# Moving a mixture's shared expert from the attention loop into the loop over the experts

## The reference

```python
x = hidden_states.reshape(T, H)
topk_idx, topk_w = _route(x, gate_weight, e_bias)
...
out = jax.ops.segment_sum(vals * flat_w[:, None], flat_t, num_segments=T)
shared = jax.nn.silu(x @ shared_gate.T) * (x @ shared_up.T) @ shared_down.T
return (out + shared).reshape(B, S, H)
```

## Time and profile before

| what | value |
|---|---|
| median of 3 runs | 1954.37 us (1952.79 to 1955.15) |
| the profiled execution | 1958.1 us, span 1956.3 us |
| PE busy | 1732.0 us, 89% of the span |
| PE weight loads | 1372.8 us, 70% |
| DVE busy | 1408.1 us, 72% |
| ACT busy | 1149.3 us, 59% |
| POOL busy | 568.1 us, 29% |

### The profile page before, as it was taken

One profiled execution on the slowest core, in us unless ns is written; L12 is line 12 of the kernel. 1 busy time (PEld: TensorE's weight loads), 2 busy tenths in 40 slices (PEclk: granted clock), 3 DMA queues, 4 the chain that ended last, 5 costly groups with the idle time before them and its releaser, 6 DMA issues.

```text
span 1956.3 us, 53909 instructions
## 1 busy us (share of the span) xinstructions
PE 1732.0 (89%) x20198; PEld 1372.8 (70%) x20208; DVE 1408.1 (72%) x4651; ACT 1149.3 (59%) x2347; POOL 568.1 (29%) x552
## 2 busy tenths in 40 slices
PE   5999999999999998588788888499999999978855
PEld 4888888888888887376667666377777777743334
DVE  4788887888888887365444443378888888859988
ACT  3666666666666664122222222378888888858875
POOL 1000000000000000388888888411112121111147
PEclk9999999999999999798999999799999999989989
DMA  3122212221222241688988887422222222203265
GB/s 98 46 66 62 66 61 70 69 66 62 64 67 62 67 121 53 173 219 200 222 208 209 211 207 171 95 67 78 67 78 67 77 70 75 67 26 149 110 234 197
DMA packets 194481, 214.04 MB, mean 109 GB/s; under 512 B 25584, under 2 KB 170352, under 8 KB 192048
## 3 DMA queue, kind: packets, MB, share of 16 engines
q1 hardware_dynamic: 169408, 171.97, 27.3%
q0 software_dynamic: 24816, 38.62, 10.9%
HBM read 125.63 MB, written 84.89 MB: 108 GB/s over the span
## 4 chain that ended last, share of the span: by engine, by line
PE 57%; DVE 19%; ACT 7%; issue 6%; DMA 5%; POOL 5%; SPq 1%; POOLq 0%; DVEq 0%; ACTq 0%
DVE mt L835 8%; PE tiles L379 7%; PE tiles L362 7%; PE bank L445 6%; ACT pt L608 6%; PE bank L524 6%; DMA xr<-token_rows,tid 4%; PE bank L408 3%; PE bank L476 3%; PE tiles L346 3%; PE bank L457 3%; PE bank L547 3%; DVE hmax L1714 2%; PE bank L1292 2%; POOL accumulator L1501 2%
## 5 line engine op out<-in xcount | busy, mean ns | idle before, releaser
L1973 POOL TENSOR_TENSOR rstd<-var,minus_half 128x2 f32<-128x2 f32 x139 | 96.9, 697 | 882.3 <-DVE var L914 869.3
L835 DVE TENSOR_REDUCE mt<-tiles 128x16 f32<-128x2048 f32 x128 | 293.5, 2293 | 69.0 <-PE tiles L362 69.0
L608 ACT ACTIVATE pt<-tiles 128x2048 f32<-128x2048 f32 x128 | 240.7, 1881 | 48.8 <-PE tiles L379 48.8
L1501 POOL DMA_INDIRECT accumulator<-ye,tid x128 | 206.0, 1610 | 47.3 <-issue 32.2
L1446 DVE TENSOR_SCALAR ye<-bank,xr 128x256 f32<-128x256 f32 x128 | 56.1, 480 | 197.2 <-PE bank L1336 163.0
L1486 POOL DMA_INDIRECT xr<-token_rows,tid x128 | 141.2, 1103 | 71.3 <-DVE within L1414 33.1
L445 PE MATMUL bank<-xt,w_q 128*128 128x128 f32 x1024 | 155.9, 286 | 0.9 <-ACT xt L616 0.9
L362 PE MATMUL tiles<-qkp 32*128 32x256 f32 x2048 | 149.1, 404 | 3.2 <-ACT qkp L630 3.0
L379 PE MATMUL tiles<-qm,qkp 32*128 32x128 f32 x4096 | 150.2, 283 | 1.4 <-DVE mt L835 1.4
L379 PEld LDWEIGHTS tiles<-qm,qkp 32*128 32x128 f32 x4096 | 125.8, 186 | 27.3 <-issue 24.6
L445 PEld LDWEIGHTS bank<-xt,w_q 128*128 128x128 f32 x1024 | 132.7, 196 | 14.7 <-issue 13.0
(11 more groups left out here) (246 smaller groups left out, 4103.5 us busy)
## 6 DMA issues: line engine op xcount, KB each, us to landing
keys_values<-res SPq DMA_DIRECT2D x64, 256.0 KB
cxax<-accumulator SPq DMA_DIRECT2D x128, 128.0 KB, 2.3
cxax<-keys_values SPq DMA_DIRECT2D x128, 128.0 KB, 2.5
hidden_away<-h_ring SPq DMA_DIRECT2D x8, 1536.0 KB, 5.0
token_rows<-pay SPq DMA_DIRECT2D x64, 160.0 KB, 1.8
pt<-in_expert_up SPq DMA_DIRECT2D x36, 256.0 KB
cxax<-in_ctx SPq DMA_DIRECT2D x64, 128.0 KB, 2.2
res<-in_x SPq DMA_DIRECT2D x64, 128.0 KB, 2.3
```

Source lines behind the costliest of these rows:

```text
L608: nc.scalar.activation(pt[r % 2][:, :, :], tiles[:, :, :], ACT.Exp).then_inc(sem("exp_done"), 1)
L835: nc.vector.tensor_reduce(mt[:, :].rearrange("p (i n c) -> p i n c", i=RT, n=2 * KC)[:, :, :, 0], tiles[:, :, :].rearrange("p i (n k) -> p ...
L1501: nc.gpsimd.indirect_dma_start(out=acc[p][:, :], out_offset=bass.IndirectOffsetOnAxis(ap=tid[b % 8][:, h:h + 1], axis=0), in_=ye[r][:, h, ...
```

## The change

Stage 1 keeps the router but no longer computes the shared expert. SP stores each batch's transposed rows in a DRAM tensor `tokens_t`, and the plain residual rows as the accumulator's initial value. In stage 2 each expert slot n also takes batch n of the shared expert: SP loads the transposed rows one slot ahead, TensorE does `shared_up` (at lag 0) and `shared_down` (at lag 1), ScalarE the tanh and the scaled output, VectorE the two products, and SP stores the output in a DRAM tensor `shared`. PSUM bank 7 holds both products in turn. In stage 3 SP loads three rows instead of two, GpSimd adds the two accumulators, and VectorE adds the shared row.

```diff
+    tokens_t = nc.dram_tensor("tokens_t", [NB, P, KC * P], f32).ap()
+    shared = nc.dram_tensor("shared_out", [T, D], f32).ap()
...
+        SHARED_IN = 3
+        sxt = [room(59 + k, 1).rearrange("p (c t) -> p c t", c=KC) for k in range(SHARED_IN)]
+        sth, ys = room(56, 1), [room(62 + k, 1) for k in range(2)]
+        sht = [room(57 + k, 1).rearrange("p (c t) -> p c t", c=FS // P) for k in range(2)]
...
-                    wait(pe, sm("silu_done"), b - 3)
...
-                wait(pe, sm("xa_done"), b)
+                wait(pe, sm("en_out"), b)
                 for c in range(KC):
                     last = nc.tensor.transpose(bank[6][:, c * P:(c + 1) * P], pay[r][:, c * P:(c + 1) * P], ident[:, :])
                 last.then_inc(sem(sm("t2_done")), 1)
...
-            def moe_up(k):
-                if k is None:
-                    return
-                b, r = k
-                p = r % 2
+            def moe_logits(k):
+                if k is None:
+                    return
+                b, r = k
                 pe.wait_ge(sem(sm("x2t_out")), b + 1)
-                pe.wait_ge(sem(sm("xt_out")), ahead(b, 5))
-                pe.wait_ge(sem("qm_done"), first + ahead(b, 4))
+                pe.wait_ge(sem(sm("x3_done")), ahead(b, 2))
                 if b == 0:
                     pe.wait_ge(sem("moe_in"), MOE_IN)
-                for n, w in enumerate((w_sg, w_su)):
-                    for j in range(FS // P):
-                        for c in range(KC):
-                            last = nc.tensor.matmul(bank[4][:, n * FS + j * P:n * FS + (j + 1) * P],
-                                                    w[:, c, j * P:(j + 1) * P], x2t[p][:, c, :],
-                                                    start=(c == 0), stop=(c == KC - 1))
-                last.then_inc(sem(sm("up_done")), 1)
-            def moe_logits(k):
-                if k is None:
-                    return
-                b, r = k
-                pe.wait_ge(sem(sm("x3_done")), ahead(b, 2))
                 for c in range(KC):
                     last = nc.tensor.matmul(bank[6][:, 256:256 + E], x2t[r % 2][:, c, :], w_gate[:, c, :],
                                             start=(c == 0), stop=(c == KC - 1))
                 last.then_inc(sem(sm("logits_done")), 1)
-            def moe_down(k):
-                if k is None:
-                    return
-                b, r = k
-                pe.wait_ge(sem(sm("silu_done")), b + 1)
-                pe.wait_ge(sem(sm("en_out")), b + 1)
-                for c in range(FS // P):
-                    last = nc.tensor.matmul(bank[6][:, 0:D], ht[r % 2][:, c, :], w_sd[:, c, :],
-                                            start=(c == 0), stop=(c == FS // P - 1))
-                last.then_inc(sem(sm("down_done")), 1)
...
                     project_v(f)
-                    moe_down(v)
                     transposes(f)
                     scores_t(k)
                     tokens_to_heads(o)
@@ -577,7 +552,6 @@
                     moe_transposes(w)
                     project_qk(f)
                     output(o)
-                    moe_up(w)
                     moe_logits(w)
                     values(k)
...
-                wait(act, sm("up_done"), b - 1)
+                wait(act, sm("logits_done"), b - 1)
+                wait(act, f"x2t_kept{r % 2}", 8 * (b - r % 2))
...
                     router_tanh(w)
-                    gate_tanh(w)
...
-                dve.wait_ge(sem(f"ax_in{p}"), 16 * (b - p) + 32)
-                nc.vector.tensor_tensor(row(b), ax[p][:, 0, :], ax[p][:, 1, :], ALU.add).then_inc(sem(sm("sum_done")), 1)
+                dve.wait_ge(sem("experts_summed"), b + 1)
+                nc.vector.tensor_tensor(row(b), row(b), ax[p][:, 0, :], ALU.add).then_inc(sem(sm("sum_done")), 1)
...
-                    shared_out(v)
...
-                    silu(w)
-                    silu_up(w)
...
+                sp.dma_start(row(b), shared[bass.ds(b * P, P), :]).then_inc(sem(f"ax_in{p}"), 16)
...
-                sp.wait_ge(sem(sm("xa_done")), b + 1)
-                sp.dma_start(acc[0][bass.ds(b * P, P), :], xa[r % 2][:, :]).then_inc(sem(f"xa_stored{r % 2}"), 16)
+                p = r % 2
+                sp.wait_ge(sem(sm("x3_done")), b + 1)
+                wait(sp, f"x3_kept{p}", 8 * (b - p))
+                sp.dma_start(acc[0][bass.ds(b * P, P), :], row(b)).then_inc(sem(f"x3_kept{p}"), 16)
                 sp.dma_start(acc[1][bass.ds(b * P, P), :], zt[:, 0, 0:D]).then_inc(sem("acc_zero"), 16)
+            def store_transposed(k):
+                if k is None:
+                    return
+                b, r = k
+                sp.wait_ge(sem(sm("x2t_out")), b + 1)
+                sp.dma_start(tokens_t[b], x2t[r % 2][:, :, :].rearrange("p c t -> p (c t)")).then_inc(sem(f"x2t_kept{r % 2}"), 16)
...
-                    store(stage(5))
+                    store(stage(4))
+                    store_transposed(stage(5))
...
+            def load_shared(e):
+                if e is None:
+                    return
+                n = e[0]
+                wait(sp, "sh_up_done", n - SHARED_IN + 1)
+                sp.dma_start(sxt[n % SHARED_IN].rearrange("p c t -> p (c t)"), tokens_t[n]).then_inc(sem(f"x2t_in{n % SHARED_IN}"), 16)
+            def keep_shared(e):
+                if e is None:
+                    return
+                n = e[0]
+                sp.wait_ge(sem("sh_out"), n + 1)
+                sp.dma_start(shared[bass.ds(n * P, P), :], ys[n % 2]).then_inc(sem(f"sh_kept{n % 2}"), 16)
             def body(stage):
+                load_shared(stage(-1))
                 load_weights(stage(0))
                 keep_pair(stage(1))
+                keep_shared(stage(2))
...
+            def shared_up(e):
+                if e is None:
+                    return
+                n = e[0]
+                pe.wait_ge(sem(f"x2t_in{n % SHARED_IN}"), 16 * (n // SHARED_IN) + 16)
+                wait(pe, "sh_out", n)
+                for m, w in enumerate((w_sg, w_su)):
+                    for j in range(FS // P):
+                        for c in range(KC):
+                            last = nc.tensor.matmul(bank[7][:, m * FS + j * P:m * FS + (j + 1) * P], w[:, c, j * P:(j + 1) * P],
+                                                    sxt[n % SHARED_IN][:, c, :], start=(c == 0), stop=(c == KC - 1))
+                last.then_inc(sem("sh_up_done"), 1)
+            def shared_down(e):
+                if e is None:
+                    return
+                n = e[0]
+                pe.wait_ge(sem("sh_silu_done"), n + 1)
+                for c in range(FS // P):
+                    last = nc.tensor.matmul(bank[7][:, 0:D], sht[n % 2][:, c, :], w_sd[:, c, :], start=(c == 0), stop=(c == FS // P - 1))
+                last.then_inc(sem("sh_down_done"), 1)
             def body(stage):
                 slot_steps(stage(-MAP_AHEAD))
                 rows_t(stage(0))
                 keys_or_values(stage(0))
+                shared_down(stage(1))
                 up(stage(1))
+                shared_up(stage(0))
                 down(stage(2))
...
+            def shared_tanh(e):
+                if e is None:
+                    return
+                n = e[0]
+                act.wait_ge(sem("sh_up_done"), n + 1)
+                wait(act, "sh_silu_done", n)
+                nc.scalar.activation(sth, bank[7][:, 0:FS], ACT.Tanh, scale=0.5).then_inc(sem("sh_th_out"), 1)
+            def shared_out(e):
+                if e is None:
+                    return
+                n = e[0]
+                act.wait_ge(sem("sh_down_done"), n + 1)
+                wait(act, f"sh_kept{n % 2}", 8 * (n - n % 2))
+                nc.scalar.activation(ys[n % 2], bank[7][:, 0:D], ACT.Copy, scale=tg_half[:, 0:1]).then_inc(sem("sh_out"), 1)
             def body(stage):
                 copy_t(stage(0))
                 copy_pair(stage(0))
+                shared_out(stage(1))
                 gate_tanh(stage(1))
+                shared_tanh(stage(0))
...
+            def shared_silu(e):
+                if e is None:
+                    return
+                n = e[0]
+                dve.wait_ge(sem("sh_th_out"), n + 1)
+                nc.vector.scalar_tensor_tensor(hs[:, :], sth, 1.0, bank[7][:, 0:FS], ALU.add, ALU.mult).then_inc(sem("sh_hs_done"), 1)
+                wait(dve, "sh_down_done", n - 1)
+                dve.wait_ge(sem("sh_hs_done"), n + 1)
+                nc.vector.tensor_tensor(sht[n % 2].rearrange("p c t -> p (c t)"), hs[:, :], bank[7][:, FS:2 * FS],
+                                        ALU.mult).then_inc(sem("sh_silu_done"), 1)
...
                 hidden(stage(1))
+                shared_silu(stage(0))
...
+            def experts_sum(b):
+                if b >= NB:
+                    return
+                p = b % 2
+                pool.wait_ge(sem(f"ax_in{p}"), 24 * (b - p) + 48)
```

(3 more changed lines are left out.)

44 lines of the change are left out of this document (9 added, 35 removed).

## The result

The changed kernel takes **2003.07 us** (median of 4 runs, 2001.14 to 2004.91) against 1953.96 for the kernel before (4 runs, 1952.79 to 1955.15): 1.0249 times, 95% interval 1.0234 to 1.0265. It is 49 us slower, where the forecast was 24 us slower.

The account below looks back on a forecast made before the run. TensorE was taken to bound the first attention, GpSimd the experts' stage until the move makes TensorE the bound there. Terms −75 − 6 + 102 + 3 = +24 us, added to the median 1954.37, gave 1978 us, range 1963 to 1996.

Parts of the forecast that it names:

- I take 1.25 … a slot of 10.34 us: First attention: each slot gets 1.25 us shorter (bounds 1.05 to 1.34), over 60 slots −75 us (−63 to −80).
- (a): First attention, behind the down product: waits for values' copy and maximum leave 0.24 of 0.86 us a slot (0 to 0.29).
- (b): First attention, behind the up products: router's logits wait for the residual; slot shorter by 1.29 us together with (a).
- at the old distances: First attention: everything behind the logits (values, next scores) follows at unchanged distances, so no added cost.
- (c): First attention's drain: the shared chain no longer stands in the router's way, −6 us (−4 to −7).
- The experts' slot: Experts' stage: TensorE paces it at 7.77 plus a 0.35 us wait for VectorE, 8.12 us a slot, +99 us.
- The tail: End of the experts' stage: a longer tail, +2 us within the stage's +102.
- The second layer: Second attention: only first slots pay a third load's issue and GpSimd's addition, +3 us (0 to 8).
- All is given back: Rival, first attention: the waits of (a) and (b) are absent, slot 8.95 us, 1895 us; chance 0.06.
- The stage absorbs more: Rival, experts' stage: no wait for the shared silu, +77 there, at best 1947, likelier about 1955 us; chance 0.09.
- The clock: Rival, experts' stage: mean grant stays 0.94, products take 8.27 us a slot, +31, 2009 us; chance 0.12.
- The port: Rival, second layer: GpSimd's addition holds VectorE's up to 0.72 us a slot, +46, 2024 us; chance 0.04.

Follow-up runs that it names:

- e1: Kernel before, with the first attention's shared down product cut to one 32-column product (shared output left out): 1944.57 us, 0.9950.
- e2: Kernel before, with the first attention's shared up products cut to one 32-column product after the first batch (shared output left out): 1902.55 us, 0.9723.
- e4: Changed kernel, with the shared up products behind the expert's down product: 1976.07 us, 1.0107.
- e5: Changed kernel without shared-expert work in the experts' stage; the second attention's third row is loaded from the input: 1893.74 us, 0.9693.
- e8: Changed kernel, with VectorE adding the two accumulators as before, no GpSimd addition, no third load (shared output left out): 2000.58 us, 1.0232.
- e9: Changed kernel, with the shared down product behind the expert's up, right ahead of the shared up products: 2032.11 us, 1.0407.
- e10: Changed kernel, with the last expert's up ahead of the shared down product in end slots that have no new expert: 1997.97 us, 1.0219.
- e11: Changed kernel with e4's and e10's edits, values ahead of the router's logits, and value projection ahead of the heads' transposes: 1919.77 us, 0.9819.
- e12: Kernel before, with values ahead of the router's logits and value projection ahead of the heads' transposes in the first attention: 1987.37 us, 1.0160.

## Why the prediction came out as it did

**The direction and both mechanisms were right.** The shared expert stood in front of two waits in the first attention, and in the experts' stage it made TensorE the bound.

**The step that failed in size: the first attention, "I take 1.25 … a slot of 10.34 us", −75.** Measured: 1.00 a slot, 60 us. The three pieces, from the slot above and the earlier trace rows:
- (a) was put at 0.24 us. The transposes start 0.15 us after the copy's end (606.97 + 0.37 = 607.34, start 607.49), not 0.05, and the scores 0.34 us behind the transposes, not 0.31; the scores start 607.83 − 604.10 = 3.73 us after the slot's first ones, where it was 3.84. So (a) gave 0.11. e1, where the same product was cut alone, shows the same: 0.15 us after the copy, and 0.12 us a slot.
- (b) was put at 1.05 us. The logits start 602.53 − 601.90 = 0.63 us after the residual starts, not 0.53: again 0.15 behind its end (602.38). They were at 675.32 − 673.74 = 1.58. So (b) gave 0.95, and e2 confirms it by itself: 0.94 us a slot.
- Behind the waits TensorE does not resume at the old distance: from the logits to the values it is 0.56 us, in e1's unwaited logits 0.49 (506.29 to 506.78). That is 0.07 more, a term that the prediction put at nothing ("at the old distances").

Together 0.11 + 0.95 − 0.07 = 0.99. The release time of 0.05 us had been read from one row of a drain slot and used for two waits of another kind; the 1.25 was inside the bounds, but the lower bound, 1.05, was not low enough. The trace of before had the right number for these very transposes. In its first slots, before the down product stands there, they wait for the same copy:

```profile
54.02 0.37 ACT L656 COPY vx<-bank 128x256 f32<-128x256 f32 x1 [0.51 <-PE bank L457]
...
54.53 0.41 PE L425 MATMUL bank<-ident,xn 128*128 128x128 f32 x2 [0.55 <-ACT vx L656]
```

The copy ends at 54.39, and the transposes start 0.14 us later.

**(c), the drain.** The remainder, 64.7 − 60 = 4.7 us of the 6, is inside its bounds, but holds the first slots too. By itself the drain, from the last maximum to the first row transposes, went from 61.98 to 54.74 us, 7.2 less; in e4, e5, e8, e9 and e10 it is 53.7 to 57.5. So (c) was about right, and the first slots returned some 2 us less than their share, which is within the 4 us that they vary by.

**The experts' slot was right: 8.12 forecast, 8.13 measured.** The last hundredths are luck, since the sum gave a wait of 0.31 and the prediction called it 0.35 without a reason. In a slot of the changed kernel, as in the earlier trace rows:

```profile
1003.13 0.28 PE L1234 MATMUL bank<-table,begun 64*128 64x130 bf16 x2
...
1005.40 0.42 DVE L1460 TENSOR_TENSOR res<-hs,bank 128x256 f32<-128x256 f32 x1
...
1005.88 1.13 PE L1320 MATMUL bank<-w_sd,res 128*128 128x256 f32 x4
```

the shared down product starts 2.75 us into the slot, the forecast's number, 0.06 us behind VectorE's second product. The list of idle time before this line (products and weight loads together, over the whole stage) names it:

```profile
  DVE res L1460: 24.3, 36
```

e4 takes exactly this wait away and leaves 7.78. The forecast's +4 for weights' transposes and a bias product and −3 for first slots can't be told apart in the 99.8.

**The tail, "+2", was mis-sized:** it took +7.5. The prediction had costed the slots and not read the drain of the stage in TensorE's new order, where the last expert's up stands behind a shared down product that waits 2.68 us and then runs at half speed. e10 gets 3.2 us of it back, e4's order 3.5, and e11, with both, is at 18.0 us from the last transposes to the last scatter-add, where before is at 15.6. The rest was not taken apart; e5 shows only that the shared work is the cause.

**The second layer, "+3",** was +0.4 in the profiled executions and 2.5 in e8. Neither can be told from the other or from nothing; its slot did not change at all.

**The rivals.** *All is given back*: refuted by e1, where 45 us were asked and 10 came. *The stage absorbs more*: refuted by the 8.13 us; it is what e4 does, by another order. *The clock*: refuted, the grant is 1.00 in the whole stage (second window above), and in e9 too, where TensorE idles for 41 of 545 us, nearly all of it in 60 waits of at most 0.7; in e5, where waits for gathers of up to 3.7 us are back, it is 0.94. The prediction's argument from the first attention was weak, since TensorE had no recorded gap there at all. The Trainium skill, "TensorE: Matmul & The Clock Gate", section "Why this matters for your kernels", puts drops down to long gaps, and the trace agrees: with the waits for gathers cut to 7.0 us the clock is full. *The port*: refuted by e8 and by the unchanged slot. The rule of the Trainium skill, "SBUF — State Buffer", section "Who interferes with whom", that weighed against the change is neither borne out nor contradicted by this: no addition of VectorE ran beside a GpSimd instruction (64 of 64), so what two such additions would cost each other no run here shows.

**Why a moved shared expert cost 49 us at first and gains 34 in the end:** as written, 2.64 us of products bought 1.00 where they left and cost 1.58 where they went. With the three waits filled by other work they buy 1.87 (11.59 − 9.72) and cost 1.23 (7.78 − 6.55). The two swaps of the first attention can't be credited with it by themselves: on the kernel before they cost 30 us (e12).

## What to carry to other kernels

Work that leaves a saturated engine can stand in front of waits, and then gives back only what is longer than they are: before forecasting a gain, list for the instruction behind it what it needs and when that is ready. Then ask in the same breath which independent group could stand there instead; here one swapped line was worth 46 us, nearly the whole loss. Read the drain slots of a pipeline in the new order too, and take the time from a releaser's end to the start from a wait of the same kind, several of them if there are several.

## What was not expected of the hardware

- The distance from a releaser's end to TensorE's start isn't one number: 0.05 us in the earlier trace rows and 0.06 at the shared down product, but 0.15 at both waits of the first attention. It isn't the length of the gap: 0.41 to 0.67 us of idling stand before starts of 0.15 (e1 and after), 0.73 before one of 0.05. It goes with the number of semaphores that the trace records for the waiting product. Over the fourteen traces it is 0.05 to 0.06 us at all 2704 TensorE waits that have one recorded semaphore and an engine's instruction as releaser. With two it is 0.14 to 0.15 at the 1152 waits whose kind recurs five times or more in its trace, and less uniform at the 243 rarer ones. The wait for the residual shows both: in after, `moe_logits` waits for `x2t_out` and `x3_done`, and starts 0.15 us behind the residual; in e2 `x2t_out` is waited for ahead of the small product, and the same logits start 508.36 − (507.82 + 0.48) = 0.06 us behind it:

```profile
507.82 0.48 DVE L862 SCALAR_TENSOR_TENSOR res<-bank,tg,res 128x256 f32<-128x256 f32 x1 [0.20 <-PE bank L476]
...
508.36 0.32 PE L538 MATMUL bank<-w_gate,x2t 128*128 128x64 f32 x1 [0.44 <-DVE res L862]
```

  No run changed the number of semaphores and nothing else, and e12's value projection, for which the profile names no releaser, lies between at 0.10. So this is a reading of the traces and not a proof.
- Two gaps of 0.55 and 0.67 us in every slot of 10.59 us left the granted clock at 1.00 for 540 us; a single gap of 2.68 us in the drain took it from 1.00 to 0.50, and a product behind it took 2.07 us in place of 1.13.
